# Two Swin blocks on one core: transposes in P's banks, a bank for hidden pieces, the second MLP product two steps later

## The chip, the core and the metric

The program runs on one NeuronCore of a Trainium2 chip. TensorE (PE) multiplies and transposes, VectorE (DVE), ScalarE (ACT) and GpSimd (POOL) work on elements, and the SP queue starts the DMAs. Each engine takes its own instructions in order and waits on semaphores for the others. The metric is device time in microseconds, lower is better.

## What is computed

The input is 32 images of 192 channels and 32 x 32 pixels. Two Swin blocks follow each other: layer 0 with a shift of 4, a relative bias and a mask, layer 1 with the same shift and without bias and mask. Cut to its core:

```python
def block(x, shift, bias, mask):                 # x: (B, H, W, 192)
    h = layer_norm(x)
    h = roll(h, (-4, -4))
    q, k, v = split_heads(windows(h, 8) @ qkv_w + qkv_b)       # 12 heads of 16
    a = softmax(q @ k.T * 16 ** -0.5 + bias + mask)
    x = x + roll(unwindows(a @ v @ proj_w + proj_b), (4, 4))
    h = layer_norm(x)
    return x + gelu(h @ fc1_w + fc1_b) @ fc2_w + fc2_b         # hidden width 768
```

## The kernel before

**Tiles.** A tile is 128 tokens, two windows. An image has 8 tiles, and with two layers over 32 images there are 512 tile steps. They go in groups of four; `group_order` lists the groups, so that groups of layer 0 and layer 1 alternate. Most operands are kept as a high and a low fp16 part: an engine writes the high part and VectorE or GpSimd subtracts it from the full value for the low part. So the second product is 18 matmuls (6 hidden blocks, three pairs of parts), and `x2` or `x5` in a row is a set of such parts.

**Steps.** There is no scheduler. `run(slot)` calls each engine's own `slot(s)` for s from -6 to beyond 512, and in it the functions stand in the order in which that engine does them. Function `f(s - 2)` in slot s means that the tile two steps older is meant. In a step TensorE does: P.V of tile s-2, the v product of tile s, scores of s, projection of s-3, the transposes of P of s-1, the subtraction of the row maximum from the scores of s (`shift_scores`), the q/k product of s+3. ScalarE copies v and q/k high, takes exp, copies P high. VectorE does the row maximum, the attention residual, statistics, v low, P low, q/k low. GpSimd does the normalising, the parts of o and the image order. SP does the DMA transposes, loads and stores.

**The MLP.** It works on a whole group of four tiles, LATE = 8 steps behind. `mlp_phase(s)` gives the phase p (a group) and the place 0 to 3 of a step in it. The first product makes six hidden pieces of 128 rows by 512 tokens (`hidden(m)`, line 587, five matmuls each), four at the end of place 0 and two at the head of place 1, so 30 matmuls in a row. They alternate between the two banks of `ps_s`, which the attention scores also use; piece 0 waits for exp of the same step (`exp_done`), and piece m >= 2 for gelu of piece m-2. ScalarE does gelu (line 723), GpSimd the high part of it (line 1137), VectorE the low part (line 968). The second product (`mlp_out`, lines 600 and 602) is done tile by tile: tile 0 in place 1, tiles 1 and 2 in place 2, tile 3 in place 3, and each is followed by VectorE's residual (line 955). Tile 1's stands in ps_o, the others in ps_v, the bank of the v product. The first of them waits for the low part of piece six (`h_lo`).

**PSUM.** Eight banks: `ps_tr` for the x and y transposes, `ps_o` for P.V, `ps_qk` for q/k and projection, `ps_v`, two of `ps_s`, and two of `ps_t` for the transposes of P. Before the gelus and after them ScalarE loads a table (lines 734 and 729).

**Where a bank is shared**, a wait on its last reader stands in front of the writer. For ps_v in `v_product`:

```python
if place == 1 or p < 0 or p == 0 == place:
    ge("v_lo", n - 1)
else:
    ge("resid2", p * GROUP + (-1, None, 0, 2)[place])
```

`ge(name, n)` waits until event `name` has come for item n.

Of the kernel before, what the change touches and what calls it, by code (L numbers as in the profile page):

```python
# [140 lines left out]
def swin_program(nc, x, layers, rel_bias, ident_in, q_mask_in, k_mask_in, out):  # L141
    H2 = C // 2
    with ExitStack() as ctx:
# [10 lines left out]
        ps_tr, ps_o, ps_qk, ps_v = banks  # L154
# [60 lines left out]
        hid16 = sb("hid16", [128, 2, HC, GROUP * TOK], F16)  # L215
# [76 lines left out]
        def _(sp):  # L292
# [71 lines left out]
            def slot(s):  # L364
# [42 lines left out]
                for n, places in ((s - LATE - 2, (0, 1)), (s - LATE - 6, (2, 3))):  # L407
                    if live(n) and visit(n)[1] == 1 and n % GROUP in places:
                        ge("y_ready", rank(n) | 1)
                        store(visit(n)[0], visit(n)[2])  # L410
# [10 lines left out]
        def _(pe):  # L421
# [29 lines left out]
            def slot(s):  # L451
# [3 lines left out]
                def take_tr(reader, n):  # L455

                    ge(*tr_reader)
                    tr_reader[:] = [reader, n]

# [8 lines left out]
                def x_transpose(n):  # L468

                    _, layer, t = visit(n)  # L470
                    take_tr("x_in", rank(n))
                    ge("x_ordered", rank(n))
                    for k in range(2):
                        last = nc.tensor.transpose(ps_tr[:, k * H2:(k + 1) * H2], x_win[:, k, t * TOK:(t + 1) * TOK],
# [27 lines left out]
                def rel_scores(n):  # L502

                    _, layer, t = visit(n)
                    if place == 1:
                        ge("gelu", p * HC + HC - 1)
# [31 lines left out]
                def p_transpose(n):  # L538


                    ge("p_lo", n - 1)
                    ge("exp_done", n)
# [5 lines left out]
                def pv_product(n):  # L548


                    if mlp and place == 3:
                        ge("resid2", p * GROUP + 1)
                    else:
                        ge("o_norm", n - 1)
# [21 lines left out]
                def hidden(m):  # L576
# [3 lines left out]
                    if m == 0:  # L580
                        for n in range(p * GROUP, (p + 1) * GROUP):
                            landed(pe, "xh_in", n + AHEAD)
                        ge("exp_done", min(s, ENDS))
                    if m >= 2:
                        ge("gelu", u - 2)
                    for i, (part, blk) in enumerate(((0, 0), (3, 0), (2, 2), (1, 1), (4, 1))):
                        last = mm(ps_s[:, u % 2, :].rearrange("p (a t) -> p a t", a=GROUP),  # L587
# [4 lines left out]
                def mlp_out(n, bank):  # L592
# [3 lines left out]
                    if n % GROUP == 0:  # L596
                        ge("h_lo", p * HC + HC - 1)
# [625 lines left out]
```

## Time and profile before

| | |
|---|---|
| median of 3 runs | 4226.17 us (4218.26 to 4227.47) |
| the profiled execution | 4221.89 us, of which the span is 4220.1 us |
| busy: TensorE, VectorE, GpSimd, ScalarE | 92%, 81%, 73%, 64% of the span |
| granted TensorE clock | 1.0 in the mean, 9 tenths or more in all 40 slices |

A timeline row gives the start, the busy time and what ran. TensorE's rows are pipelined: one begins before the end of the last is over, so the time that a set takes is read from one start to the next. The same holds for VectorE, by less. Between groups of four steps the pattern repeats, with small differences between groups of layer 0 and of layer 1: the bias product (line 510) and the x transposes (line 474) come with layer 0, the y transposes (line 609) with the tiles that leave layer 1.

### The profile page before, as it was taken

The numbers are of one execution on the slowest core, as the hardware profiler recorded it, in microseconds if no ns is written. First come the engines' busy times: TensorE is split into PE (matmuls) and PEld (weight loads), VectorE is DVE, ScalarE is ACT, GpSimd is POOL, SyncE is SP. The second block draws the span as 40 slices with busy tenths as digits, with TensorE's granted clock in tenths as the row PEclk, the third lists the DMA queues.
The fourth block names the chain that finished last, engine by engine and source line by source line (L and its number), as shares of the span: only waits on it lengthen the run. The fifth ranks groups of instructions, "written<-read, shape, count | busy, mean of one in ns | idle before, by whom it ended". The sixth has DMA issues, their size and how long they took to land. (4 is left out here: it accounts for less than half of the span.)

```text
span 4220.1 us, 173918 instructions
## 1 busy us (share of the span) xinstructions
PE 3900.1 (92%) x65872; PEld 2870.6 (68%) x65872; DVE 3430.2 (81%) x9093; ACT 2692.4 (64%) x5409; POOL 3085.5 (73%) x6257
## 2 busy tenths in 40 slices
PE   4999999999999999999999999999999999999998
PEld 2667667766766766766676676667666766766765
DVE  6888888888888888888888888888888888888885
ACT  1666666666666666666666666666666666666665
POOL 4777777777777777777777777777777777777775
PEclk9999999999999999999999999999999999999999
DMA  4644545445554554555546555445544555544543
GB/s 104 108 95 101 103 98 101 104 100 99 103 103 97 104 101 98 103 99 104 98 101 103 99 100 100 104 96 105 102 96 103 101 102 100 100 103 96 95 98 63
DMA packets 1545145, 421.00 MB, mean 100 GB/s; under 512 B 1441782, under 2 KB 1542522, under 8 KB 1544316
## 3 DMA queue, kind: packets, MB, share of 16 engines
q1 hardware_dynamic: 1540732, 409.87, 49.9%
q8 instruction: 528, 8.65, 0.9%
q14 instruction: 301, 2.47, 0.2%
q10 hardware_dynamic: 3584, 0.01, 0.0%
HBM read 32.15 MB, written 25.17 MB: 14 GB/s over the span
## 5 line engine op out<-in xcount | busy, mean ns | idle before, releaser
L968 DVE TENSOR_TENSOR hid<-scaled,hid 128x512 f16<-128x512 f32 x768 | 674.1, 891 | 344.9 <-POOL hid L1137 325.5
L600 PE MATMUL bank<-w_fc,hid 128*128 128x192 f16 x9216 | 845.4, 246 | 106.9 <-DVE hid L968 104.8
L587 PE MATMUL ps_s<-xh,w_fc 128*128 128x512 f16 x3840 | 859.2, 379 | 70.9 <-ACT stage L709 64.5
L1074 POOL TENSOR_TENSOR rstd<-vare,half 128x2 f32<-128x2 f32 x520 | 360.6, 693 | 770.1 <-DVE vare L908 770.1
L600 PEld LDWEIGHTS bank<-w_fc,hid 128*128 128x128 f16 x9216 | 761.4, 98 | 195.9 <-DVE v_blk L924 169.6
L587 PEld LDWEIGHTS ps_s<-xh,w_fc 128*128 128x128 f16 x3840 | 355.5, 97 | 560.5 <-issue 110.9
L1137 POOL TENSOR_SCALAR hid<-scaled 128x512 f16<-128x512 f32 x768 | 564.7, 739 | 121.8 <-ACT scaled L723 120.9
L723 ACT ACTIVATE scaled<-ps_s,b_fc 128x512 f32<-128x512 f32 x768 | 529.3, 689 | 154.5 <-PE ps_s L587 133.7
L690 ACT ACTIVATE xs<-xn 128x192 f16<-128x192 f32 x512 | 185.7, 363 | 683.2 <-POOL xn L1081 683.2
L715 ACT ACTIVATE pt<-ps_t 128x768 f16<-128x768 f32 x512 | 415.7, 812 | 303.8 <-PE ps_t L544 300.7
L463 PE MATMUL bank<-w_qkv,xh 128*128 128x384 f16 x2560 | 501.0, 326 | 6.1 <-DMA xh<-xs 3.6
L709 ACT ACTIVATE stage<-ps_s 128x768 f32<-128x768 f32 x512 | 417.4, 815 | 134.6 <-PE ps_s L533 134.6
L930 DVE TENSOR_REDUCE smax<-ps_s 128x12 bf16<-128x768 f32 x512 | 488.3, 954 | 16.8 <-PE ps_s L524 1.5
L935 DVE TENSOR_TENSOR pt<-ps_t,pt 128x768 f16<-128x768 f32 x512 | 489.6, 956 | 12.1
L696 ACT ACTIVATE qk<-bank 128x768 f16<-128x768 f32 x512 | 419.7, 820 | 9.7 <-PE bank L463 9.7
L704 ACT ACTIVATE v_blk<-bank 64x192 f16<-64x192 f32 x1024 | 333.7, 326 | 137.2 <-PE bank L496 131.0
L561 PEld LDWEIGHTS bank<-v_blk,pt 128*64 128x64 f16 x18432 | 333.0, 112 | 128.8 <-issue 95.9
L544 PE MATMUL ps_t<-ident,stage 128*128 128x128 f32 x3072 | 419.7, 273 | 0.1
L914 DVE SCALAR_TENSOR_TENSOR qk<-bank,qk 128x192 f16<-128x192 f32 x1024 | 315.8, 350 | 91.7 <-ACT qk L696 88.8
L561 PE MATMUL bank<-v_blk,pt 128*64 128x34 f16 x18432 | 383.5, 185 | 5.0 <-DVE pt L935 4.7
L463 PEld LDWEIGHTS bank<-w_qkv,xh 128*128 128x128 f16 x2560 | 244.6, 97 | 180.2 <-DVE x_tok L955 8.3
L924 DVE SCALAR_TENSOR_TENSOR v_blk<-bank,v_blk 64x192 f16<-64x192 f32 x1024 | 357.0, 349 | 7.1
(113 smaller groups left out, 7182.7 us busy)
## 6 DMA issues: line engine op xcount, KB each, us to landing
x_img<-in_x_dram SPq DMA_DIRECT2D x256, 96.0 KB, 2.2
out_dram<-y_img SPq DMA_DIRECT2D x256, 96.0 KB, 2.0
xh<-xs SPq DMA_TRANSPOSE x520, 2.5
qkt<-qk SPq DMA_TRANSPOSE x512, 3.3
ot<-os SPq DMA_TRANSPOSE x512, 2.3
stage<-in_L_conv_fc_w_dram SPq DMA_DIRECT2D x2, 384.0 KB, 4.3
stage<-in_L_conv_w_fc_dram SPq DMA_DIRECT2D x2, 384.0 KB, 4.2
stage<-in_L_conv_qkv_w_dram SPq DMA_DIRECT2D x2, 288.0 KB
```

The source lines that it names most:

```text
L463: last = mm(dst, blocks[:, blk, :], w[:, part, n0:n1], start=(i == 0), stop=(i == 4 and bias is None))
L544: last = nc.tensor.transpose(ps_t[:, g // 3, (g % 3) * TOK:(g % 3 + 1) * TOK], p_tok[:, n % 2, g].rearrange("p a k -> p (a k)"), ident[:, :])
L561: last = mm(ps_o[rows, g * 2 * VW:(g + 1) * 2 * VW].rearrange("p (a d) -> p a d", a=2), pt[:, n % 2, ps, g, rows], v_blk[:, n % 2, vs, :, ...
L587: last = mm(ps_s[:, u % 2, :].rearrange("p (a t) -> p a t", a=GROUP), w_fc1[layer][:, part, m * 128:(m + 1) * 128], xh[:, p % 2 * GROUP:(p ...
L600: mm(bank[:, 0:C], hid16[:, hs, m, tok], w_fc2[layer][:, ws, m, :], start=(m == 0 and i == 0), stop=False)
L696: copy(hi_places(n), src.broadcast_to([128, 2, HEADS, 2, HD]), ACT.Copy, scale=UNSCALE)\
L709: nc.scalar.activation(p_tok[:, n % 2].rearrange("p g a k -> p a g k"), ps_s[:, :, 0:PAIRS * WIN].rearrange("p a (g k) -> p a g k", g=PAIR ...
L723: nc.scalar.activation(hid[:, u % 4, :], ps_s[:, u % 2, :], ACT.Gelu, bias=b_fc1[layer][:, m:m + 1], scale=UNSCALE).then_inc(S["gelu"], 1)
L930: v.tensor_reduce(smax[:, n % 2], ps_s[:, :, 0:PAIRS * WIN].rearrange("p a (g k) -> p a g k", g=PAIRS), AX.X, ALU.max).then_inc(S["max_don ...
L935: v.tensor_tensor(pt[:, n % 2, 1].rearrange("p (b g) t -> p b (g t)", b=2), ps_t[:, :, 0:3 * TOK], pt[:, n % 2, 0].rearrange("p (b g) t -> ...
L968: v.tensor_tensor(hid16[:, 1, m, :], hid[:, u % 4, :], hid16[:, 0, m, :], ALU.subtract)\
L1137: g_.tensor_scalar(hid16[:, 0, m, :], hid[:, u % 4, :], 1.0, 0.0, ALU.mult, ALU.add)\
```

## The change

- `ps_tr` is gone as a bank for transposes. The x transposes now write P's first bank (`ps_x`), the y transposes P's second (`ps_y`). They wait until P's low part of the step before is made, and P's transposes wait for their readers in turn.
- The freed bank `ps_hid` takes hidden pieces 0 and 5; pieces 1 to 4 alternate in `ps_s`. Piece 0 no longer waits for exp, piece 1 does. Pieces 0 to 2 stand at the end of place 0, pieces 3 to 5 in place 1 behind P.V and v.
- The second product of tile n is in step n + 10 (`OUT = LATE + 2`), one in every step, always in ps_v; its residual opens VectorE's next step. So `v_product` waits for the residual of the step before in every place. `hid16` becomes two buffers, the second in the memory of the weight stage.
- VectorE's statistics of the attention output, both aggregates and the centring stand together behind v low; in place 1 P's low part comes before them. Low parts of hidden pieces 0 to 4 are in place 1, of piece 5 in place 2.
- ScalarE copies x and y at the head of the step; its q/k copy comes before gelu 0.
- The group order begins each round with layer 0 instead of layer 1, and the stores are in one place, four steps after the second product.

```diff
+OUT = LATE + 2
...
-        order += [(image - 2, 1, 0), (image, 0, 0), (image - 2, 1, 1), (image, 0, 1)]
+        order += [(image, 0, 0), (image - 2, 1, 0), (image, 0, 1), (image - 2, 1, 1)]
...
-        ps_tr, ps_o, ps_qk, ps_v = banks
+        ps_hid, ps_o, ps_qk, ps_v = banks
+        hid_banks = [ps_hid[:, :], ps_s[:, 0, :], ps_s[:, 1, :], ps_s[:, 0, :], ps_s[:, 1, :], ps_hid[:, :]]
+        ps_x = ps_t[:, 0, 0:C]
+        ps_y = ps_t[0:H2, 1, 0:2 * TOK].rearrange("p (k t) -> p k t", k=2)
...
@@ TensorE, x_transpose
-                    take_tr("x_in", rank(n))
+                    ge("p_lo", min(n - 8, ENDS))
+                    ge("x_in", rank(n) - 1)
...
@@ v_product
-                    if place == 1 or p < 0 or p == 0 == place:
+                    if n <= OUT:
                         ge("v_lo", n - 1)
                     else:
-                        ge("resid2", p * GROUP + (-1, None, 0, 2)[place])
+                        ge("resid2", n - OUT - 1)
...
@@ hidden
+                        ge("gelu", u - 1)
+                    if m == 1:
                         ge("exp_done", min(s, ENDS))
-                    if m >= 2:
-                        ge("gelu", u - 2)
+                    if m >= 3:
+                        ge("gelu", u - (2, 2, 5)[m - 3])
...
@@ mlp_out
                     if n % GROUP == 0:
-                        ge("h_lo", p * HC + HC - 1)
+                        ge("h_lo", n // GROUP * HC + HC - 1)
+                    ge("v_lo", min(s, ENDS))
+                    ge("resid2", n - 1)
...
@@ y_transpose
-                    take_tr("y_ready", rank(n))
+                    ge("p_lo", min(s - 2, ENDS))
+                    ge("y_ready", rank(n) - 1)
...
@@ TensorE's step
-                if mlp and place == 1:
-                    hidden(4)
-                    hidden(5)
                 if live(s + 6) and visit(s + 6)[1] == 0:
                     x_transpose(s + 6)
+                if live(s - OUT - 2) and visit(s - OUT - 2)[1] == 1:
+                    y_transpose(s - OUT - 2)
                 if live(s) and place != 1:
                     rel_scores(s)
                 if live(s - 2):
                     pv_product(s - 2)
                 if live(s):
                     v_product(s)
+                if mlp and place == 1:
+                    for m in range(3, HC):
+                        hidden(m)
...
                 if live(s + 3):
                     qk_product(s + 3)
+                if live(s - OUT):
+                    mlp_out(s - OUT)
                 if mlp and place == 0:
                     for m in range(3):
                         hidden(m)
...
@@ VectorE's step
+                if live(s - OUT - 1):
+                    mlp_residual(s - OUT - 1)
...
-                if mlp and place == 1:
-                    hidden_lo(5)
...
+                if mlp and place == 1:
+                    hidden_lo(4)
+                if mlp and place == 1 and live(s - 1):
+                    p_lo(s - 1)
+                if mlp and place == 2:
+                    hidden_lo(5)
```

TensorE, a group whose tiles are of layer 1, from the q/k product of place 0 to that of place 1. Names: `ps_s<-xh,w_fc` hidden pieces, `bank<-v_blk,pt` P.V, `bank<-w_qkv,xh 64x96` v, `bank<-w_fc,hid` the second product. Before:

```order
L463 MATMUL bank<-w_qkv,xh 128x384 x5
L587 MATMUL ps_s<-xh,w_fc 128x512 x30
L474 MATMUL bank<-ident,x_win 128x96 x2
L561 MATMUL bank<-v_blk,pt 64x34 x36
L496 MATMUL bank<-w_qkv,xh 64x96 x20
L524 MATMUL ps_s<-qkt 64x64 x24
L463 MATMUL bank<-w_proj,ot 128x192 x5
L465 MATMUL bank<-b_out,bias_rows 128x192
L544 MATMUL ps_t<-ident,stage 128x128 x6
L533 MATMUL ps_s<-smax,neg_ident 128x384 x2
```

And after:

```order
L607 MATMUL bank<-w_fc,hid 128x192 x18
L609 MATMUL bank<-b_out,bias_rows 128x192
L592 MATMUL bank<-xh,w_fc 128x512 x5
L592 MATMUL ps_s<-xh,w_fc 128x512 x10
L476 MATMUL ps_t<-ident,x_win 128x96 x2
L564 MATMUL bank<-v_blk,pt 64x34 x36
L498 MATMUL bank<-w_qkv,xh 64x96 x20
L592 MATMUL ps_s<-xh,w_fc 128x512 x10
L592 MATMUL bank<-xh,w_fc 128x512 x5
L526 MATMUL ps_s<-qkt 64x64 x24
```

The thirty matmuls are two sets of fifteen with the x transposes, P.V and v between them, and a second product stands ahead of the first set.

VectorE, one plain step from the MLP residual (`x_tok<-bank`) to the q/k low part; `smax` is the row maximum, `mv` and `bn` the statistics, `nmean` and `vare` the centring, `pt` P's low part. Before:

```order
L955 SCALAR_TENSOR_TENSOR x_tok<-bank,x_tok 128x192
L888 BN_STATS bn<-x_tok 128x6
L894 BN_AGGR mv<-bn 128x2
L941 RECIPROCAL o_inv<-bank 128x12
L948 TENSOR_TENSOR o_tok<-bank,o_inv 128x192
L930 TENSOR_REDUCE smax<-ps_s 128x12
L955 SCALAR_TENSOR_TENSOR x_tok<-bank,x_tok 128x192
L888 BN_STATS bn<-x_tok 128x6
L924 SCALAR_TENSOR_TENSOR v_blk<-bank,v_blk 64x12x16 x2
L894 BN_AGGR mv<-bn 128x2
L907 TENSOR_SCALAR nmean<-mv 128x2
L908 TENSOR_SCALAR vare<-mv 128x2
```

And after:

```order
L871 BN_STATS bn<-x_tok 128x6
L938 SCALAR_TENSOR_TENSOR x_tok<-bank,x_tok 128x192
L924 RECIPROCAL o_inv<-bank 128x12
L931 TENSOR_TENSOR o_tok<-bank,o_inv 128x192
L913 TENSOR_REDUCE smax<-ps_s 128x12
L938 SCALAR_TENSOR_TENSOR x_tok<-bank,x_tok 128x192
L907 SCALAR_TENSOR_TENSOR v_blk<-bank,v_blk 64x12x16 x2
L871 BN_STATS bn<-x_tok 128x6
L877 BN_AGGR mv<-bn 128x2 x2
L890 TENSOR_SCALAR nmean<-mv 128x2
L891 TENSOR_SCALAR vare<-mv 128x2
```

The statistics that stood behind the MLP residual now stand ahead of it, and the first aggregate went from there to behind v low.

## Rows read from the trace of the kernel before

**Rows 1.** The page: span, and each engine's busy time and share.
```profile
span 4220.1 us, 173918 instructions
...
PE 3900.1 (92%) x65872; PEld 2870.6 (68%) x65872; DVE 3430.2 (81%) x9093; ACT 2692.4 (64%) x5409; POOL 3085.5 (73%) x6257
```

**Rows 2.** TensorE's timeline: start us, busy us, engine line op, tiles, count [idle before].
```profile
1999.58 6.71 PE L587 MATMUL ps_s<-xh,w_fc 128*128 128x512 f16 x30 [0.56 <-ACT stage L709]
...
2063.61 6.71 PE L587 MATMUL ps_s<-xh,w_fc 128*128 128x512 f16 x30 [0.56 <-ACT stage L709]
```

**Rows 3.** The page's groups by line: busy, mean ns, idle before them.
```profile
L968 DVE TENSOR_TENSOR hid<-scaled,hid 128x512 f16<-128x512 f32 x768 | 674.1, 891 | 344.9 <-POOL hid L1137 325.5
L600 PE MATMUL bank<-w_fc,hid 128*128 128x192 f16 x9216 | 845.4, 246 | 106.9 <-DVE hid L968 104.8
```

**Rows 4.** TensorE's timeline, one plain step (place 3 to place 0).
```profile
2021.59 0.60 PE L496 MATMUL bank<-w_qkv,xh 128*64 128x96 f16 x20
2022.12 0.38 PE L524 MATMUL ps_s<-qkt 64*64 64x64 f16 x24
...
2023.59 0.38 PE L609 MATMUL bank<-ident,x_tok 128*96 128x128 f32 x2
2023.81 0.49 PE L533 MATMUL ps_s<-smax,neg_ident 128*128 128x384 bf16 x2
...
2024.95 1.65 PE L600 MATMUL bank<-w_fc,hid 128*128 128x192 f16 x18
...
2026.52 0.49 PE L510 MATMUL ps_s<-bias_tab,pair_ident 128*128 128x384 f16 x2
2026.94 0.75 PE L561 MATMUL bank<-v_blk,pt 128*64 128x34 f16 x36
2027.53 0.60 PE L496 MATMUL bank<-w_qkv,xh 128*64 128x96 f16 x20
```

**Rows 5.** VectorE's timeline in the same step.
```profile
2021.11 0.36 DVE L955 SCALAR_TENSOR_TENSOR x_tok<-bank,x_tok 128x192 f32<-128x192 f32 x1 [0.32 <-PE bank L602]
2021.38 0.35 DVE L888 BATCH_NORM_STATS2 bn<-x_tok 128x6 f32<-128x192 f32 x1
...
2022.56 0.96 DVE L930 TENSOR_REDUCE smax<-ps_s 128x12 bf16<-128x768 f32 x1
...
2023.82 0.36 DVE L888 BATCH_NORM_STATS2 bn<-x_tok 128x6 f32<-128x192 f32 x1
2024.10 0.71 DVE L924 SCALAR_TENSOR_TENSOR v_blk<-bank,v_blk 64x192 f16<-64x192 f32 x2
2024.84 0.18 DVE L894 BATCH_NORM_AGGREGATE mv<-bn 128x2 f32<-128x6 f32 x1
...
2025.19 0.16 DVE L908 TENSOR_SCALAR vare<-mv 128x2 f32<-128x2 f32 x1
2025.38 0.96 DVE L935 TENSOR_TENSOR pt<-ps_t,pt 128x768 f16<-128x768 f32 x1
2026.49 0.62 DVE L914 SCALAR_TENSOR_TENSOR qk<-bank,qk 128x192 f16<-128x192 f32 x2
2027.03 0.35 DVE L955 SCALAR_TENSOR_TENSOR x_tok<-bank,x_tok 128x192 f32<-128x192 f32 x1
```

**Rows 6.** ScalarE's timeline: gelu six, exp's table load, P's copy.
```profile
2006.32 0.69 ACT L723 ACTIVATE scaled<-ps_s,b_fc 128x512 f32<-128x512 f32 x1 [0.39 <-PE ps_s L587]
...
2008.30 1.28 ACT L729 ACT_TABLE_LOAD   x1
...
2009.82 0.81 ACT L715 ACTIVATE pt<-ps_t 128x768 f16<-128x768 f32 x1
```

**Rows 7.** VectorE's timeline: the last hidden low part of a group.
```profile
2011.11 0.69 DVE L968 TENSOR_TENSOR hid<-scaled,hid 128x512 f16<-128x512 f32 x1
```

**Rows 8.** GpSimd's rstd and ScalarE's copy of xn, timelines of each.
```profile
2018.85 0.69 POOL L1074 TENSOR_TENSOR rstd<-vare,half 128x2 f32<-128x2 f32 x1 [1.37 <-DVE vare L908]
...
2021.28 0.36 ACT L690 ACTIVATE xs<-xn 128x192 f16<-128x192 f32 x1 [0.75 <-POOL xn L1081]
```

More of the change, by code:

```diff
@@ L406, in slot @@
                     load(visit(s + 9)[0] + 1, visit(s + 9)[2])
[L407 to L410, printed above, removed]
+                n = s - OUT - 4
+                if live(n) and visit(n)[1] == 1:
+                    ge("y_ready", rank(n) | 1)
+                    store(visit(n)[0], visit(n)[2])
             run(slot)
@@ L548, in pv_product @@
                 def pv_product(n):
[L551 to L554, printed above, removed]
+                    ge("o_norm", n - 1)
                     ge("v_lo", n)
@@ L722, in gelu @@
                     ge("h_lo", u - 4)
-                    nc.scalar.activation(hid[:, u % 4, :], ps_s[:, u % 2, :], ACT.Gelu, bias=b_fc1[layer][:, m:m + 1],
+                    nc.scalar.activation(hid[:, u % 4, :], hid_banks[m], ACT.Gelu, bias=b_fc1[layer][:, m:m + 1],
                                          scale=UNSCALE).then_inc(S["gelu"], 1)
@@ L742, in y_evac @@
                             act.wait_ge(y_stored[h], 16 * image)
-                    tile = ps_tr[0:H2, 0:2 * TOK].rearrange("p (k t) -> p k t", k=2)
-                    for win, img in box_pairs(t, tile, y_img[:, :, :]):
+                    for win, img in box_pairs(t, ps_y, y_img[:, :, :]):
                         last = copy(img, win, ACT.Copy)
@@ L763, in slot @@
                 if mlp and place == 1:
+                    for m in range(3, HC):
+                        gelu(m)
                     load_exp()
@@ L776, in slot @@
                     load_gelu()
-                    gelu(0)
                 if live(s + 3):
@@ L780, in slot @@
                 if mlp and place == 0:
+                    gelu(0)
                     gelu(1)
-                if last_block and place == 2:
-                    y_evac(p * GROUP + 1)
             run(slot)
@@ L959, in attention_residual, with mlp_residual @@
                     residual(n, ps_qk[:, 0:C], stream(n, 1), stream(n, 0), "pr", "resid1")
-                def mlp_residual(n, bank):
-                    residual(n, bank[:, 0:C], token_rows(n), stream(n, 1), "fc2", "resid2")
+                def mlp_residual(n):
+                    residual(n, ps_v[:, 0:C], token_rows(n), stream(n, 1), "fc2", "resid2")
                 def hidden_lo(m):
@@ L1143, in slot @@
                     norm1_lo(s + 4)
[L1144 to L1145 removed]
                 if live(s - 4):
                     norm2_lo(s - 4)
+                if mlp and place == 1:
+                    hidden_hi(3)
                 if live(s + 3):
                     set_mask(s + 3)
[L1150 to L1151 removed]
                 if live(s - 2):
@@ L1154, in slot @@
                     o_lo(s - 2)
+                if mlp and place == 1:
+                    hidden_hi(4)
+                    hidden_hi(5)
                 if live(s + 10) and visit(s + 10)[1] == 0 and s + 10 >= TILES:
@@ L1163, in slot @@
                 if mlp and place == 0:
-                    for m in range(4):
+                    for m in range(3):
                         hidden_hi(m)
```

103 lines of the change are left out of this document (35 added, 68 removed).

## The prediction, made before the changed kernel was run

> **What bounds the kernel now.** I read the page's busy shares first. TensorE is busy for 92% of the span and VectorE for 81% [rows 1], which looks like a TensorE kernel that can win 8% at most. The share hides where each waits, so the timeline comes next. The starts of the six hidden pieces repeat every 64.0 us per two groups (1999.58 to 2063.61) [rows 2]. TensorE idles 0.56 us before the first piece, for exp. The groups by line show that the second product (L600) waited 104.8 us for VectorE's low part of the hidden layer, 0.8 us in each of 128 groups [rows 3].
>
> Then one plain step, a step without hidden pieces. On TensorE it runs from one v product to the next, 2021.59 to 2027.53, 5.94 us [rows 4]. On VectorE the same step, from one MLP residual to the next, takes 5.92 us (2021.11 to 2027.03) and has next to no gap in it [rows 5]. So here VectorE is a second bound, as tight as TensorE. They are tied in a ring through the bank ps_v: residual, v product, scores, row maximum, the rest of VectorE's step, next residual. The price of the change is decided in this ring.
>
> **What the change takes away.** In a group TensorE stood 0.56 us before piece one (the exp), 0.8 us before the first L600. Now piece one has a bank of its own and a second product stands before it, and the second product comes two steps later. Both waits go: 1.4 us a group, 87 us over 62 pairs of groups, if nothing else were late. No matmul, activation or VectorE operation is added or dropped; the steady numbers of each stay.
>
> **What is late next.** I walk one group on the new order, from the start of the row maximum in place 0.
>
> Stretch A, to the end of piece six, is TensorE's. Row maximum to the subtraction of it 1.00 (0.96 plus a handover); subtraction and q/k product 1.14 (2023.81 to 2024.95); second product with bias 1.57 (2024.95 to 2026.52) [rows 4]; three pieces 3.27, half of the 6.71 for six less an end of 0.17 [rows 2]; a transpose pair 0.22 (2023.59 to 2023.81), which I take for x too; P.V 0.59; v 0.53; three more pieces 3.27. Sum 11.59. The gelus finish behind: piece four needs gelu two, with P.V and v between as cover, so I put no wait here. If that cover failed, gelu's 0.69 would show.
>
> Stretch B, from there to the row maximum of place 2, is no longer TensorE's. ScalarE must do gelu six, load exp's table and then copy P before VectorE can take P's low part. Handover 0.20 and gelu 0.69; 1.54 from its end to P's copy (load at 2008.30, copy at 2009.82); copy 0.81 [rows 6]; handover 0.03. VectorE: P low 0.88 to the next start, its 0.96 less the 0.08 by which back-to-back operations overlap (0.36 at 2023.82, next start 2024.10); statistics, two aggregates and centring 1.00 (that 0.28, then 0.54 from the aggregate at 2024.84 to P low at 2025.38, and 0.18 for the second aggregate, which now stands beside the first); q/k low 0.54 (2026.49 to 2027.03); statistics 0.28; residual 0.36 and handover 0.06; v, scores and handover 0.97 (2021.59 to 2022.56) [rows 4, 5]. Sum 7.36. TensorE's own work in B up to v is about 4.8 to 5.7, so it waits about 0.7 to 1.6 in front of v. Before, the gelus stood a whole first half of a step earlier and this was hidden. The removed waits thus come back at another place.
>
> Stretch C, place 2 to place 3, is the ring plus hidden piece six on VectorE. The ring costs more than before. Row maximum and attention residual 1.26 (2022.56 to 2023.82), v low 0.74, statistics to centring 1.00, P low 0.88, q/k low 0.54, statistics 0.28, residual and handover 0.42, then 0.97 to the next row maximum: 6.09 [rows 5]. Before it was 5.92, since statistics for a later tile (2021.38) stood behind the residual and, with an aggregate, filled the time in which VectorE waited for v and scores. Now it stands in front of the residual, and only reciprocal and normalisation fill that hole. That is 0.17 a step. Low part six is in the ring in place 2: alone it takes 0.61 to the next start (2011.11, busy 0.69) [rows 7]. The mean of all 768 is 0.89 [rows 3]; those beside GpSimd work are the long ones. In B the centring came late, so GpSimd's chain of place 2 (o high, o low) falls upon it. Bounds are 0.61 and 0.89; I take 0.89, nearer to the mean. C is 6.98.
>
> What the row shows is a low part that grows by 0.20 beside GpSimd, on average over all. The Trainium skill, "SBUF — State Buffer", "Who interferes with whom", says more: a VectorE instruction with two SBUF inputs and a GpSimd instruction that reads SBUF lock each other out for the whole instruction. By that rule low part six might stand a whole GpSimd operation longer and C would be some 0.3 longer. The sum goes without it.
>
> Stretch D, place 3 to place 0, is the plain ring, 6.09.
>
> A group is 11.59 + 7.36 + 6.98 + 6.09 = 32.02. Every second group adds something. Where the tiles are of layer 0, TensorE has x pair, y pair, bias and P.V (0.22 + 0.22 + 0.42 + 0.59, the bias from 2026.52 to 2026.94) between P's low part and v [rows 4], since both transposes now wait in P's bank for that low part. With a handover 1.5 against VectorE's 1.17 for q/k low, statistics and residual: +0.4 in place 3 and +0.1 in place 0. The x transposes were free of that wait before. So a pair is 64.54 against 64.03, +0.51 over 62 pairs (some 125 of the 128 groups run in the steady state), +32 us. Warm-up gets the same wait in some eight steps, and the tail has two more steps but the same four second products behind the last low part: together I take +3, between 0 and +8. The profiled execution took 4221.9 us (span 4220.1) [rows 1], so the sum is 4257. The median of the three runs is 4226.2, 0.1% above that execution; I say 4258.
>
> Also moved: the store on SP's queue comes four steps after the second product for all places, and GpSimd's hidden part four goes from place 0 to place 1. SP's stores wait on y that ScalarE made in the step before, and nothing behind them on SP is needed for more than a step. Piece four's high part has VectorE's earlier low parts beside it. I cost both at nothing; if GpSimd were late, the row maximum in place 1 would show it. ScalarE's q/k copy now stands behind the gelu table load in place 0; VectorE then idles over 1 us there, but A belongs to TensorE in that time.
>
> One more rule bears on B. The row shows the table load at 2008.30 and P's copy 1.52 later [rows 6]. The Trainium skill, "ScalarE: Activation LUTs", "What ACT_TABLE_LOAD costs", adds a drain of about 1.38 us to each switch. With it B would be 1.4 longer, +170 us in all; the trace has no such gap between the load and the copy, and the measurement decides.
>
> **Rivals.**
>
> (1) The ring takes 6.09, but low part six runs alone (0.61). A pair is 0.56 less, 63.98: 4222 - 3 + 3 = 4222. For it: in every second group GpSimd has no image work then. Against: its o low comes right there. This is "no change".
>
> (2) Faster. TensorE keeps what the removed waits give, because VectorE's moved pieces cost nothing: ring 5.92 in C and D as in the trace, low part six alone, so 63.98 - 4 x 0.17 = 63.3 a pair, -0.73 x 62 + 3 = -42: 4180. For it: VectorE has 19% idle, and it has no more to do than before. Against: that idle lies in places 0 and 1, where it is not the bound. It decides if the row maximum in a plain step starts sooner than 6.0 after the last.
>
> (3) Slower still. In place 2 ScalarE's copy of xn (L690) stands before v's copy. It came 2.43 us after GpSimd's rstd started (2018.85 to 2021.28) [rows 8]. Centring in place 1 now comes behind P low, so I compare two paths from the last centring operation to v low in place 2. VectorE's: 0.19 + 0.54 + 0.28 + 0.42 + 0.97 + 1.26 = 3.66 [rows 5]. The other: about 0.3 to rstd, 2.43, xn's copy 0.3 and v's two copies 0.6 (estimates from the 0.36 of xn's), 3.6 to 3.7: no slack. If GpSimd is later by 0.3, v low and all behind it is later by 0.3: +0.6 a pair, +37 us, 4295.
>
> (4) The change doesn't take effect as told: banks or order coincide with the old ones. The order lists show that they don't; under 1 in 50.
>
> **Chances and range.** Forecast 4258 (4235 to 4275): 0.42. Rival 1: 0.20. Rival 2, with in-between sizes: 0.22. Rival 3: 0.16. A measurement of this kernel can tell about 0.2%, 8 us, from no change. From the cases: faster by more than that 0.25, within it 0.20, slower 0.55. The range 4178 to 4302 takes in rivals 1 and 3 and nearly all of 2.
>
> **What would show it.** The wait of the second product for the hidden low part falls from 104.8 to under 80 us and sits in place 2; the wait of piece one for exp is gone. PEld or TensorE waits for the MLP residual in front of v grow to about 1 us per group in place 2, and plain steps take 6.1 us on VectorE. In the six-piece stretch there is no gap over 0.2. VectorE's low part six in place 2 shows whether 0.69 or 0.96. I am wrong if plain steps come under 6.0, or if v in place 2 starts before 6.2 after the last piece's end.

## The result, and the profile after

The changed kernel took 4242.39 us (median of 4 runs, 4241.56 to 4242.92) against 4224.76 for the kernel before: a ratio of 1.0044, 95% interval 1.0026 to 1.0061. The forecast was slower, 4258, range 4178 to 4302. The direction held, and so did the mechanism in its main terms; the size came out 16 us smaller. Three of the signs named beforehand failed. Two are the "I am wrong if" thresholds, both crossed by a little: a plain step comes at 5.98 us (under 6.0), and v in place 2 starts 6.10 us after the last piece's end (under 6.2). The third failed plainly: the second product waits for the hidden low part more than before, not less. (Pieces one to six are `hidden(0)` to `hidden(5)` here, as in the prediction.)

The page of the kernel after, its span, busy shares and four groups by line; they answer [rows 1] and [rows 3].

```profile
span 4241.1 us, 174413 instructions
...
PE 3931.5 (93%) x65872; PEld 2899.8 (68%) x65872; DVE 3377.8 (80%) x9093; ACT 2688.4 (63%) x5409; POOL 3111.0 (73%) x6257
...
L913 DVE TENSOR_REDUCE smax<-ps_s 128x12 bf16<-128x768 f32 x512 | 490.2, 957 | 147.8 <-PE ps_s L526 136.4
...
L607 PE MATMUL bank<-w_fc,stage 128*128 128x192 f16 x4608 | 422.7, 246 | 60.1 <-DVE stage L951 58.7
L607 PE MATMUL bank<-w_fc,hid 128*128 128x192 f16 x4608 | 422.7, 246 | 58.6 <-DVE hid L951 58.0
...
L907 DVE SCALAR_TENSOR_TENSOR v_blk<-bank,v_blk 64x192 f16<-64x192 f32 x1024 | 363.2, 355 | 35.6 <-ACT v_blk L697 28.8
```

The counts of each engine's operations are those of before: no work was added. The wait of the second product is 58.7 + 58.0 = 116.7 us (before 104.8), and two waits are new in size: VectorE's row maximum waits 136.4 us for the scores (1.5 before), and v's low part 28.8 us for ScalarE's copy of v. Two rows of the waits view (who <- for whom: us in all, times, longest):

```profile
PE bank L498 <- DVE x_tok L938: 77.5, 135, 1.3
DVE v_blk L907 <- ACT v_blk L697: 28.8, 123, 1.0
```

The first is v's product waiting for the MLP residual. To see which of these lie on the path, one reads VectorE's row maxima. A row maximum (L930 before, L913 after) can start only when both engines have come round, so its starts cut the pair of groups into eight stages. VectorE's timeline of the kernel before, the stages from place 2 to place 3 and from place 3 to place 0 in both groups:

```profile
2913.26 0.96 DVE L930 TENSOR_REDUCE smax<-ps_s 128x12 bf16<-128x768 f32 x1
2920.66 0.96 DVE L930 TENSOR_REDUCE smax<-ps_s 128x12 bf16<-128x768 f32 x1
2926.60 0.96 DVE L930 TENSOR_REDUCE smax<-ps_s 128x12 bf16<-128x768 f32 x1
...
2945.57 0.96 DVE L930 TENSOR_REDUCE smax<-ps_s 128x12 bf16<-128x768 f32 x1
2953.03 0.96 DVE L930 TENSOR_REDUCE smax<-ps_s 128x12 bf16<-128x768 f32 x1
2958.73 0.96 DVE L930 TENSOR_REDUCE smax<-ps_s 128x12 bf16<-128x768 f32 x1
```

And of the kernel after, one whole pair, with the idle time before each in brackets:

```profile
2911.91 0.96 DVE L913 TENSOR_REDUCE smax<-ps_s 128x12 bf16<-128x768 f32 x1
2924.43 0.96 DVE L913 TENSOR_REDUCE smax<-ps_s 128x12 bf16<-128x768 f32 x1 [0.56 <-PE ps_s L526]
2930.66 0.96 DVE L913 TENSOR_REDUCE smax<-ps_s 128x12 bf16<-128x768 f32 x1 [0.20 <-PE ps_s L526]
2938.21 0.96 DVE L913 TENSOR_REDUCE smax<-ps_s 128x12 bf16<-128x768 f32 x1
2944.19 0.96 DVE L913 TENSOR_REDUCE smax<-ps_s 128x12 bf16<-128x768 f32 x1 [0.26 <-PE ps_s L526]
2956.33 0.96 DVE L913 TENSOR_REDUCE smax<-ps_s 128x12 bf16<-128x768 f32 x1 [0.23 <-PE ps_s L526]
2962.88 0.96 DVE L913 TENSOR_REDUCE smax<-ps_s 128x12 bf16<-128x768 f32 x1 [0.46 <-PE ps_s L526]
2970.05 0.96 DVE L913 TENSOR_REDUCE smax<-ps_s 128x12 bf16<-128x768 f32 x1 [0.46 <-PE ps_s L526]
2976.23 0.96 DVE L913 TENSOR_REDUCE smax<-ps_s 128x12 bf16<-128x768 f32 x1
```

The same starts, read between 2890 and 2990 us in each kernel and subtracted (the last column is the sum, a pair of groups). Stage 0-1 and 1-2 together are the prediction's A and B, 2-3 is C, 3-0 is D.

| kernel | 0-1 | 1-2 | 2-3 | 3-0 | 0-1 | 1-2 | 2-3 | 3-0 | pair |
|---|---|---|---|---|---|---|---|---|---|
| before | 12.17 | 6.31 | 7.40 | 5.94 | 12.16 | 6.81 | 7.46 | 5.70 | 63.95 |
| after | 12.52 | 6.23 | 7.55 | 5.98 | 12.14 | 6.55 | 7.17 | 6.18 | 64.32 |
| e1_stat | 12.51 | 6.10 | 7.67 | 5.81 | 12.14 | 6.28 | 7.18 | 6.23 | 63.92 |
| e2_vfirst | 12.52 | 6.22 | 6.96 | 5.97 | 12.14 | 6.54 | 6.69 | 6.17 | 63.21 |
| e3_bias | 12.52 | 6.22 | 7.23 | 5.98 | 12.14 | 6.55 | 7.18 | 5.97 | 63.79 |
| e4_all | 12.52 | 6.11 | 6.70 | 5.83 | 12.14 | 6.29 | 6.80 | 5.93 | 62.32 |
| e5_twice5 | 12.52 | 6.22 | 8.17 | 5.97 | 12.14 | 6.54 | 7.89 | 6.17 | 65.62 |
| e9_spare | 12.52 | 6.49 | 7.57 | 5.98 | 12.14 | 6.82 | 7.19 | 6.17 | 64.88 |
| e8_before_v | 11.89 | 6.35 | 7.40 | 5.94 | 12.00 | 6.82 | 7.45 | 5.70 | 63.55 |

(Starts are rounded, so a stage may be 0.01 off. In the kernel before and in e8_before_v, the halves may stand the other way round; only their sums are compared. One stretch can mislead: over 60 pairs of each trace the median stages are within 0.02 of these rows in all but two places. The 6.80 of e4_all is rare, the median there is 6.35; and where e1_stat has 6.23 the median is 6.17.) From before to after, stages 0-1 and 1-2 together stay at 37.45 and 37.44, the 2-3 stages give 0.14 back, and the plain stages 3-0 lose 0.52: 11.64 becomes 12.16. That is the answer to "where did the time go". In 0-1 and 1-2 the gone waits (0.56 for exp, 0.8 for the low part) pay for most of a second product, 1.57, that has moved to place 0. In 2-3 TensorE has one second product less, but VectorE's ring does not let the stage shrink by more than 0.07. In 3-0, where nothing was to be won, the ring is longer. The means over 60 pairs say the same: -0.05 in 0-1 and 1-2, -0.18 in 2-3, +0.52 in 3-0.

Two stretches lie outside the pairs. The first hidden piece starts at 146.42 us instead of 140.92, so the warm-up costs 5.5. The last block of hidden pieces starts at 4217.80, and the end comes 23.3 us later; before, it was 23.4 (4196.73 to 4220.1). The tail is unchanged:

```profile
4217.80 1.24 PE L592 MATMUL bank<-xh,w_fc 128*128 128x512 f16 x5
```

The 127 groups between these two starts take 4071.4 us instead of 4055.8, 15.6 more. With the 5.5 this is the 21.0 by which the two profiled spans differ; the medians of the runs differ by 17.6.

### The profile page after: what moved, and what is told of

Same layout as the page of the kernel before. It is cut to its first block, busy times and chain, and to the rows that moved or that the text cites. A ratio compares the mean times of both kernels' runs of the same rounds, so it can differ in the third digit from the quotient of the medians.

```text
span 4241.1 us, 174413 instructions
## 1 busy us (share of the span) xinstructions
PE 3931.5 (93%) x65872; PEld 2899.8 (68%) x65872; DVE 3377.8 (80%) x9093; ACT 2688.4 (63%) x5409; POOL 3111.0 (73%) x6257
## 4 chain that ended last, share of the span: by engine, by line
PE 57%; DVE 15%; ACT 11%; issue 9%; POOL 4%; DVEq 0%; DMA 0%; POOLq 0%; SPq 0%; ACTq 0%
PE ps_s L592 13%; PE bank L607 9%; PE bank L464 7%; PE bank L592 6%; PE bank L564 5%; PE bank L498 4%; PE ps_t L550 4%; ACT L722 4%; DVE pt L918 3%; DVE bn L871 2%; ACT scaled L716 2%; ACT pt L708 2%; POOL rstd L1059 2%; PE ps_s L526 2%; PE ps_s L535 2%
## 5 line engine op out<-in xcount | busy, mean ns | idle before, releaser
L913 DVE TENSOR_REDUCE smax<-ps_s 128x12 bf16<-128x768 f32 x512 | 490.2, 957 | 147.8 <-PE ps_s L526 136.4
L592 PE MATMUL ps_s<-xh,w_fc 128*128 128x512 f16 x2560 | 595.6, 380 | 0.0
L683 ACT ACTIVATE xs<-xn 128x192 f16<-128x192 f32 x512 | 186.5, 364 | 627.1 <-POOL xn L1066 627.0
L716 ACT ACTIVATE scaled<-ps_s,b_fc 128x512 f32<-128x512 f32 x512 | 351.7, 687 | 216.0 <-PE ps_s L592 216.0
L607 PE MATMUL bank<-w_fc,stage 128*128 128x192 f16 x4608 | 422.7, 246 | 60.1 <-DVE stage L951 58.7
L607 PE MATMUL bank<-w_fc,hid 128*128 128x192 f16 x4608 | 422.7, 246 | 58.6 <-DVE hid L951 58.0
L607 PEld LDWEIGHTS bank<-w_fc,stage 128*128 128x128 f16 x4608 | 382.5, 98 | 109.7 <-DVE stage L951 83.2
L607 PEld LDWEIGHTS bank<-w_fc,hid 128*128 128x128 f16 x4608 | 382.7, 98 | 108.2 <-DVE hid L951 82.4
L592 PEld LDWEIGHTS ps_s<-xh,w_fc 128*128 128x128 f16 x2560 | 240.1, 98 | 280.1
L689 ACT ACTIVATE qk<-bank 128x768 f16<-128x768 f32 x512 | 409.8, 800 | 10.6 <-PE bank L464 10.5
L951 DVE TENSOR_TENSOR stage<-scaled,stage 128x512 f16<-128x512 f32 x384 | 318.4, 829 | 110.7 <-POOL stage L1122 65.0
L951 DVE TENSOR_TENSOR hid<-scaled,hid 128x512 f16<-128x512 f32 x384 | 312.2, 813 | 106.0 <-POOL hid L1122 64.3
L907 DVE SCALAR_TENSOR_TENSOR v_blk<-bank,v_blk 64x192 f16<-64x192 f32 x1024 | 363.2, 355 | 35.6 <-ACT v_blk L697 28.8
```

Source lines behind the costliest of these rows:

```text
L592: last = mm(hid_banks[m].rearrange("p (a t) -> p a t", a=GROUP), w_fc1[layer][:, part, m * 128:(m + 1) * 128], xh[:, p % 2 * GROUP:(p % 2 ...
L607: mm(ps_v[:, 0:C], hid16[n // GROUP % 2][:, hs, m, tok], w_fc2[layer][:, ws, m, :], start=(m == 0 and i == 0), stop=False)
L689: copy(hi_places(n), src.broadcast_to([128, 2, HEADS, 2, HD]), ACT.Copy, scale=UNSCALE)\
L716: nc.scalar.activation(hid[:, u % 4, :], hid_banks[m], ACT.Gelu, bias=b_fc1[layer][:, m:m + 1], scale=UNSCALE).then_inc(S["gelu"], 1)
L913: v.tensor_reduce(smax[:, n % 2], ps_s[:, :, 0:PAIRS * WIN].rearrange("p a (g k) -> p a g k", g=PAIRS), AX.X, ALU.max).then_inc(S["max_don ...
L951: v.tensor_tensor(hid16[p % 2][:, 1, m, :], hid[:, u % 4, :], hid16[p % 2][:, 0, m, :], ALU.subtract)\
```

## Experiments

Each is an edit of the changed kernel, except the last. Differences to it are differences of medians, and each ratio is to the kernel before, timed beside it. The kernel before had medians of 4221.9 to 4224.8 us in these timings, so a difference of 3 us says nothing.

**Where VectorE's statistics stand (e1_stat).**

```diff
@@ VectorE's step
                 if live(s - OUT - 1):
                     mlp_residual(s - OUT - 1)
+                if live(s + 5):
+                    statistics(s + 5, 0)
...
-                if live(s + 6):
-                    statistics(s + 6, 0)
```

> One part of the change undone on VectorE: the statistics for a later tile stand behind the MLP residual again, as before, so the residual starts some 0.27 us sooner and the hole in front of the row maximum is filled. Theory A (VectorE's ring residual - v - scores - row maximum sets places 2 and 3): each ring gets 0.27 us shorter where q/k low and residual come last, that is in four of six ring steps per pair of groups (not where transposes and bias stand between P low and v): about -1.1 us a pair, -60 to -70 us, 4175 to 4185 us. Theory B (TensorE sets the steps, VectorE's order is slack): within 5 us of the changed kernel, 4242.

Measured: 4217.43 us, ratio 0.9987 (0.9978 to 0.9997), 25 us less than the changed kernel. The sign and the mechanism are right: row maxima wait 74.3 us for scores instead of 136.4, and the plain step without transposes goes from 5.98 to 5.81, the 0.17 of the prediction (this run's own expectation said 0.27 a ring). The size was missed: 4217 lies between both theories. In the table, 1-2 gains 0.40 over both groups, but 2-3 gives 0.13 of it back and the 3-0 stage with transposes gains nothing. The reason for the first is in VectorE's timeline of e1_stat, place 2:

```profile
2944.91 0.96 DVE L913 TENSOR_REDUCE smax<-ps_s 128x12 bf16<-128x768 f32 x1 [0.20 <-PE ps_s L526]
...
2946.61 0.73 DVE L907 SCALAR_TENSOR_TENSOR v_blk<-bank,v_blk 64x192 f16<-64x192 f32 x2 [0.47 <-ACT v_blk L697]
```

v's low part waits 0.47 for ScalarE's copy, where it waited 0.22 in the changed kernel (in all 52.8 us against 28.8), and the stage takes 7.18 where 0.17 less than 7.17 was to be had. What VectorE saves before the row maximum it spends in front of v. So there is a third path, and it hangs on ScalarE's order.

**ScalarE's order in a step (e2_vfirst).** The copy of v (L697) goes ahead of the copy of xn (L683), which waits for GpSimd.

```diff
@@ ScalarE's step
+                if live(s):
+                    v_hi(s)
                 if live(s - 4):
                     norm2_hi(s - 4)
-                if live(s):
-                    v_hi(s)
```

> ScalarE makes v's high part before its copy of xn. Theory A (rival 3 of the prediction at work: in place 2 v low waits for v's copy, which stands behind the copy of xn, 28.8 us in total in the trace): the wait goes, -20 to -30 us, 4212 to 4222 us. Theory B (the wait is covered, since the end of that step is set by the transposes behind P low): within 5 us of 4242.

Measured: 4183.11 us, ratio 0.9908 (0.9893 to 0.9923), 59 us less, twice what was expected. The table puts all of it in stage 2-3: 7.55 to 6.96 and 7.17 to 6.69. ScalarE's timeline of the changed kernel and then of e2_vfirst, place 2 of a group:

```profile
2963.37 0.36 ACT L683 ACTIVATE xs<-xn 128x192 f16<-128x192 f32 x1 [3.10 <-POOL xn L1066]
2963.64 0.65 ACT L697 ACTIVATE v_blk<-bank 64x192 f16<-64x192 f32 x2
```

```profile
2063.01 0.67 ACT L697 ACTIVATE v_blk<-bank 64x192 f16<-64x192 f32 x2 [1.00 <-PE bank L498]
2063.82 0.36 ACT L683 ACTIVATE xs<-xn 128x192 f16<-128x192 f32 x1
```

In the first, ScalarE idles 3.10 us for GpSimd and cannot take v, which has long been in its bank when xn comes; v's copy ends at 2964.29, and VectorE has waited 0.22 for it. In the second, v's copy ends 0.34 after the row maximum of its step has begun (2063.34). So v's low part starts 0.26 after the attention residual instead of 0.56, which gives back 0.30. The other half goes with contention, and VectorE's and GpSimd's timelines show it. First the changed kernel (GpSimd, then VectorE), then e2_vfirst (VectorE, then GpSimd):

```profile
2030.72 0.55 POOL L1095 TENSOR_TENSOR os<-o_tok,os 128x192 f16<-128x192 f32 x1
```

```profile
2030.07 0.73 DVE L907 SCALAR_TENSOR_TENSOR v_blk<-bank,v_blk 64x192 f16<-64x192 f32 x2 [0.22 <-ACT v_blk L697]
2030.84 0.98 DVE L951 TENSOR_TENSOR hid<-scaled,hid 128x512 f16<-128x512 f32 x1
```

```profile
2064.47 0.72 DVE L907 SCALAR_TENSOR_TENSOR v_blk<-bank,v_blk 64x192 f16<-64x192 f32 x2
2065.23 0.69 DVE L951 TENSOR_TENSOR hid<-scaled,hid 128x512 f16<-128x512 f32 x1
```

```profile
2065.42 0.91 POOL L1095 TENSOR_TENSOR os<-o_tok,os 128x192 f16<-128x192 f32 x1
```

In the changed kernel GpSimd's o part is under way (since 2030.72) when low part six starts at 2030.84, and low part six takes 0.98. In e2_vfirst GpSimd comes at the same point of the step, but v's low part is 0.30 earlier, so VectorE is first, by 0.19 us, and takes 0.69. GpSimd's operation is now the longer one (0.91 instead of 0.55), where nobody waits for it. This is the rule and not one group: low part six takes about 0.98 in 125 of the 128 groups of the changed kernel (0.69 in all 128 of the kernel before) and 0.69 in 126 of e2_vfirst. So a wait of 0.22 had cost 0.5 to 0.6 us, once in every group of 32 us. The second product's waits for that low part fall from 116.7 to 21.4 + 20.4 = 41.8 us.

**TensorE's order in front of v (e3_bias).** Bias ahead of the transposes that wait for P's low part.

```diff
@@ TensorE's step
+                if live(s) and place != 1:
+                    rel_scores(s)
                 if live(s + 6) and visit(s + 6)[1] == 0:
                     x_transpose(s + 6)
                 if live(s - OUT - 2) and visit(s - OUT - 2)[1] == 1:
                     y_transpose(s - OUT - 2)
-                if live(s) and place != 1:
-                    rel_scores(s)
```

> TensorE does the bias product of layer 0 before the x and y transposes, which wait for P low; the bias product doesn't. Theory A (in place 3 of layer 0 groups, and by a little in place 0, the work between P low and v sets the step): 0.42 us less in one step and 0.1 us in another per pair of groups, -25 to -32 us, 4210 to 4217 us. Theory B (the MLP residual comes last there too): within 5 us of 4242.

Measured: 4209.96 us, ratio 0.9972 (0.9961 to 0.9983), 32 us less. Two stages changed, 7.55 to 7.23 and 6.18 to 5.97, together the 0.53 of the pair. This is the term "+0.4 in place 3 and +0.1 in place 0" measured, as 0.32 and 0.21; its sum was right, and it came only from the order of the two functions.

**All three (e4_all).**

> The three edits at once: statistics behind the residual, v's high part before the copy of xn, bias before the transposes. Theory A: with the bias out of the way the residual is last in more steps, so the parts add up to at least their sum, about -2 us a pair of groups: 4110 to 4140 us, faster than both kernels. Theory B (something behind them, the exp table load or the matmuls themselves, takes over): less than two thirds of the sum of the single gains.

Measured: 4117.51 us (4114.29 to 4117.92), ratio 0.975 (0.9736 to 0.9765). It is 125 us below the changed kernel; the three alone sum to 117. They help each other: in most pairs the second 2-3 stage is 6.35 where e2_vfirst has 6.69, and with the bias out of the way the second 3-0 stage goes from 6.18 to 5.93. How much of this each edit gives was not separated. Part of the gain is lost again. The median stages add up to 61.86, the mean pair is 62.40, and nearly all of the difference lies in the 0-1 and 3-0 stages of some groups, where TensorE's projection now waits for the DMA of o (`ot<-os`): 26.7 us in 59 waits, against 1.3 us in 3 in the changed kernel. The page of e4_all:

```profile
PE 3890.1 (95%) x65872; PEld 2901.9 (71%) x65872; DVE 3346.8 (81%) x9093; ACT 2731.4 (66%) x5409; POOL 3137.1 (76%) x6257
```

This beats both kernels, by 2.5% and 2.9%. What the change removed is 104.8 us of waits for the low part [rows 3] and 64.5 us for exp, this row of the waits view of the kernel before:

```profile
PE ps_s L587 <- ACT stage L709: 64.5, 117, 0.6
```

Together 169 us, of which e4_all keeps 104 (4117.51 against 4221.86 for the kernel before, timed beside it). So the removed waits were worth something; the three orders of instructions around them cost 125.

**One low part doubled, in place 2 and in place 1 (e5_twice5, e6_twice0).** The same VectorE operation is done twice, once into a spare tile. For piece six it stands in the ring, for piece one in a place where VectorE waits anyway.

```diff
+        twice = sb("twice", [128, GROUP * TOK], F16)
...
@@ hidden_lo, e5_twice5 (in e6_twice0 the condition is m == 0)
+                    if m == 5:
+                        v.tensor_tensor(twice[:, :], hid[:, u % 4, :], hid16[p % 2][:, 0, m, :], ALU.subtract)
```

> VectorE does the low part of hidden piece six twice, in place 2; the second result goes to a spare tile. Nothing else changes and the output stays. Theory A (place 2 is VectorE's ring, and whatever is added there is paid in full): 0.6 to 0.95 us in each of 128 groups, +77 to +120 us over the changed kernel's 4242: 4320 to 4362 us. Theory B (VectorE's 20% idle absorbs it): under +15 us.

> The same doubling for the low part of piece one, at the head of place 1. Theory A (the stretch up to the row maximum of place 1 is TensorE's, VectorE waits there 0.5 us or so three times): under +15 us, 4242 to 4257 us. Theory B (VectorE is the bound throughout): +77 us or more, as for piece six.

Measured: 4328.76 us, ratio 1.0254 (1.0239 to 1.0269), 86 more than the changed kernel; and 4245.16 us, ratio 1.0058 (1.0041 to 1.0075), 3 more. The groups of e5_twice5 (VectorE, by line) and then of e6_twice0, 64 of each of two names:

```profile
L953 DVE TENSOR_TENSOR twice<-scaled,hid 128x512 f16<-128x512 f32 x64 | 62.4, 975 | 1.9
```

```profile
L953 DVE TENSOR_TENSOR twice<-scaled,hid 128x512 f16<-128x512 f32 x64 | 44.6, 698 | 31.6 <-POOL hid L1125 31.6
```

Equal work on the same engine costs 86 us in place 2 and 3 in place 1. In place 2 the stages grow by 0.62 and 0.72 (8.17 and 7.89). That is less than the 0.98 that its row shows. Of the two low parts in a row only the first takes 0.98; the second takes 0.68 and 0.77 in turn, 0.60 and 0.69 to the next start, and that is what the added one costs. This shows that VectorE's chain sets the time in place 2, and that its 20% of idle time lies elsewhere.

**ScalarE's chain behind the gelus (e9_spare).** Stretch B was forecast as ScalarE's and VectorE's, not TensorE's. Three more one-element activations stand between the table load and P's copy.

```diff
-        spare = sb("spare", [1, 2], F32)
+        spare = sb("spare", [1, 8], F32)
...
@@ load_exp
+                    for i in range(2, 5):
+                        nc.scalar.activation(spare[:, i:i + 1], half[0:1, :], ACT.Exp)
```

> ScalarE does three more one-element exps after the table load of place 1, which delays its copy of P by about 0.1 us each. Theory A (stretch B is set by gelu six, table load and P's copy): the delay is paid in full, 0.3 us in each of 128 groups, +30 to +45 us over 4242: 4272 to 4287 us. Theory B (VectorE's low parts or TensorE set stretch B): under +10 us.

Measured: 4279.30 us, ratio 1.0137 (1.0122 to 1.0152), 37 more. ScalarE's timeline of the changed kernel, then of e9_spare, in place 1:

```profile
2955.99 0.69 ACT L716 ACTIVATE scaled<-bank,b_fc 128x512 f32<-128x512 f32 x1 [0.39 <-PE bank L592]
2956.70 1.28 ACT L722 ACT_TABLE_LOAD   x1
...
2958.10 0.78 ACT L708 ACTIVATE pt<-ps_t 128x768 f16<-128x768 f32 x1
```

```profile
2004.40 1.28 ACT L723 ACT_TABLE_LOAD   x1
2005.69 0.39 ACT L723 ACTIVATE spare<-half 1x1 f32<-1x1 f32 x3
...
2006.08 0.78 ACT L708 ACTIVATE pt<-ps_t 128x768 f16<-128x768 f32 x1
```

P's copy starts 1.68 us after the table load instead of 1.40. The 0.28 shows in full: stage 1-2 grows by 0.26 and 0.27, and 128 x 0.28 = 36 us. The chain of B goes through ScalarE's table load and P's copy, with no slack at all.

**The wait for exp (e7_expwait).** Piece one (`hidden(0)`) waits for exp again, though it has its own bank.

```diff
@@ hidden
                         ge("gelu", u - 1)
-                    if m == 1:
                         ge("exp_done", min(s, ENDS))
```

> The wait of hidden piece one for exp is put back, though its bank doesn't need it. Theory A (the second product that now stands in front of the pieces covers the exp anyway, so the bank of its own removes nothing more): within 5 us of the changed kernel, 4242. Theory B (the free bank is what took the 0.56 us a group away): up to +72 us.

Measured: 4245.64 us, ratio 1.0057 (1.0042 to 1.0072), 3 more than the changed kernel, which is not told from none; its stages 0-1 take 12.14 and 12.52 again. So it was not the freedom of its bank from exp that removed the 0.56 us; the second product, 1.57 us that now stands ahead of piece one, covers exp.

**A like edit on the kernel before (e8_before_v).** ScalarE's copy of v ahead of xn's. In this kernel the copy of xn stood further up, so the edit also puts it behind gelus five and six and the copy of x in place 1.

```diff
@@ ScalarE's step, kernel before
-                if live(s - 4):
-                    norm2_hi(s - 4)
                 if mlp and place == 1:
                     gelu(4)
                     gelu(5)
...
                 if live(s):
                     v_hi(s)
+                if live(s - 4):
+                    norm2_hi(s - 4)
```

> The kernel before, with one edit that gained 59 us on the changed kernel: ScalarE makes v's high part before its copy of xn. Theory A (that queueing is a side effect of the change, which moved the centring behind P low in place 1; in the kernel before v low hardly waited, 7 us in all): within 8 us of before, 4222 to 4226. Theory B (the edit is good by itself): 1% faster here too, about 4180 us.

Measured: 4226.85 us against 4222.54, ratio 1.001 (1.0000 to 1.0019): no gain in time. In the stages 2-3, where the edit gave 0.59 and 0.48 in the changed kernel, it gives nothing here (7.40 and 7.45). So that cost was made by the change, which put the centring in place 1 behind P's low part and so made xn late.

But the edit is not idle here. The median 0-1 stages are 0.28 and 0.16 shorter. In the groups shown below, GpSimd waits for xn's copy before its low part of xn, so that operation no longer falls beside VectorE's hidden low part four. VectorE in the kernel before and in e8_before_v, then GpSimd and TensorE in e8_before_v:

```profile
2007.70 0.95 DVE L968 TENSOR_TENSOR hid<-scaled,hid 128x512 f16<-128x512 f32 x1 [0.29 <-POOL hid L1137]
```

```profile
2009.49 0.69 DVE L968 TENSOR_TENSOR hid<-scaled,hid 128x512 f16<-128x512 f32 x1 [0.29 <-POOL hid L1137]
```

```profile
2010.54 0.55 POOL L1115 TENSOR_TENSOR xs<-xn,xs 128x192 f16<-128x192 f32 x1 [1.15 <-ACT xs L690]
```

```profile
2063.87 0.57 PE L463 MATMUL bank<-w_proj,ot 128*128 128x192 f16 x5 [0.66 <-DMA ot<-os]
```

The last row is what takes the gain away again. GpSimd's parts of o come later too (10.46 us after the start of piece one instead of 9.71), and TensorE's projection waits for their DMA: 23.0 us in 33 waits, against 1.8 in one. The median stages add up to 63.55 instead of 63.95, but the mean pair is 64.07, against 64.13. That the late parts of o make the DMA late is read from these rows, not tested.

## Why the prediction was right, and where not

**A, 11.59.** Right. From the row maximum at 2944.19 to the end of piece six. That end is gelu six's start less the handover of 0.20: 2955.99 - 0.20 = 2955.79, so 11.60. TensorE's timeline of the changed kernel has no bracket in it:

```profile
2947.93 1.24 PE L592 MATMUL bank<-xh,w_fc 128*128 128x512 f16 x5
2949.01 2.32 PE L592 MATMUL ps_s<-xh,w_fc 128*128 128x512 f16 x10
...
2954.71 1.24 PE L592 MATMUL bank<-xh,w_fc 128*128 128x512 f16 x5
```

The gelus were hidden, as costed.

**B, 7.36.** Right in kind, too long by 0.27. Measured 2955.79 to 2962.88, 7.09. The mis-sized terms: gelu six to P's copy took 2.11, not 0.69 + 1.54 (the same table load was followed by P's copy 1.52 after its start before, and 1.40 now; the rows don't show why); and the statistics up to the centring took 0.90 where 1.00 was taken, since q/k low starts 0.07 behind `vare`, where 0.19 was read for P's low part. The rest agrees within some 0.03 a term. v's product does wait for the residual, 0.98, as said "about 1 us a group in place 2":

```profile
2961.89 0.62 PE L498 MATMUL bank<-w_qkv,xh 128*64 128x96 f16 x20 [0.98 <-DVE x_tok L938]
```

The threshold named beforehand was that v starts no sooner than 6.2 after the last piece's end. It was 2961.89 - 2955.79 = 6.10, so this sign failed, by the same mis-sized terms.

**C, 6.98 and 7.38.** Too short by 0.19 and 0.17 (7.17 and 7.55). Here rival 3 came partly true. From the attention residual to v low 0.38 was taken; in D it is 0.27, here 0.57 (2963.75 to 2964.32):

```profile
2963.75 0.35 DVE L938 SCALAR_TENSOR_TENSOR x_mid<-bank,x_new 128x192 f32<-128x192 f32 x1
2964.32 0.73 DVE L907 SCALAR_TENSOR_TENSOR v_blk<-bank,v_blk 64x192 f16<-64x192 f32 x2 [0.22 <-ACT v_blk L697]
2965.08 0.98 DVE L951 TENSOR_TENSOR stage<-scaled,stage 128x512 f16<-128x512 f32 x1
2965.98 0.35 DVE L871 BATCH_NORM_STATS2 bn<-x_mid 128x6 f32<-128x192 f32 x1
```

The prediction called that path "no slack" at a price of 0.3 and gave it 0.16; e2_vfirst confirms the mechanism and shows that the price was 0.5, because the wait also decides who comes first at low part six. That low part took 0.90 to the next start; 0.89 was taken, so rival 1 (0.61) is out in this kernel, and is what e2_vfirst makes true.

**D, 6.09 and 6.19.** Measured 5.98 and 6.18. The claim that a statistics operation on the wrong side of the residual costs 0.17 was right: it came out as 0.17 when undone in the one plain stage without transposes. Before to after the plain stages grew by 0.52 a pair; e3_bias takes 0.21 of that away, e3_bias and e1_stat's edit together (e4_all) 0.40. The level was 0.11 too high, all of it in the 0.38 behind the attention residual. In [rows 5] the operation behind it is a statistics that reads its result; now it is v low, which does not, and it starts after 0.27. "I am wrong if plain steps come under 6.0" was set too tight: one comes at 5.98, against 5.70 for the shortest before, so rival 2 (5.92 kept, pair 63.3) did not come about.

**The sum.** The groups forecast 64.54 a pair; the clean pair shows 64.32: A and B -0.46, C +0.36, D -0.12. Before, the forecast's base of 64.03 holds (63.95 in this stretch). The measured mean over all groups from 5 to 121 rose by 0.28 a pair, from 64.13 to 64.41, and 62 x 0.28 = 17 us, where the forecast had 32. The 0.22 that a pair is under the forecast is B and D, costed too long, less C, costed too short. That these errors partly cancel is luck. The clean pair's +0.37 would be 23; part of the difference is that the kernel before has some pairs with longer 2-3 stages than this one (up to 8.83 instead of 7.40).

One figure beside the sum is wrong. "1.4 us a group, 87 us over 62 pairs" counts the 1.4 once a pair. The two waits come in every group, 104.8 + 64.5 = 169 us in all. The forecast did not use the 87; it was added up from the stretches.

**The wait of the second product.** Wrong: "falls from 104.8 to under 80". It is 116.7. The step that failed is the reading of the removed 0.8 us as a wait that goes. It sits in place 2 now:

```profile
2966.11 1.66 PE L607 MATMUL bank<-w_fc,stage 128*128 128x192 f16 x18 [0.90 <-DVE stage L951]
```

0.90 us in nearly every group. It costs nothing by itself, as far as the rows show: VectorE's residual, which needs this product, waited for TensorE 7 times in the whole run, 12.3 us. TensorE has less to do in place 2 than VectorE, whose ring sets the step, and the idle time has to appear somewhere. The prediction's own sum for C implied it; the sign named for it did not follow from the sum. Before a wait is counted as gone, ask what the engine would wait for next.

**Bank and store.** The moved store, GpSimd's hidden part four and ScalarE's q/k copy were costed at nothing; the stages leave no room for a large term, but none of the three was tested alone. Warm-up and tail together were taken as +3, between 0 and +8, and were +5.5 and -0.1.

**The rule on the shared port.** The rows show low part six at 0.98 when GpSimd started an operation of 0.55 just before it, with 0.43 of that left, and at 0.69 when VectorE started first, by 0.19; then GpSimd's grew from 0.55 to 0.91. The Trainium skill, "SBUF — State Buffer", "Who interferes with whom", says that whoever comes first holds the port and the other blocks. The order agrees with the trace. The amount doesn't quite: a full block would have added 0.43 to VectorE's and the row shows 0.29; it would have added 0.50 to GpSimd's, and the row shows 0.36. **The table load.** P's copy starts 1.40 after the load's start, 0.12 after its end. The drain that the Trainium skill, "ScalarE: Activation LUTs", "What ACT_TABLE_LOAD costs", adds to each switch is not in these rows, and e9_spare shows that a gap there would have been felt in full.

## What to carry to other kernels

When two engines are tied in a ring, cut the timeline at an instruction that both must reach (here the row maximum) and compare the stages; a removed wait counts only in a stage where its engine is the later one. After a change of order, look in every in-order queue for an instruction that waits and has ready work behind it: one copy queued behind another cost 1.4% in the changed kernel, in a stage where the kernel before had no such cost. A total that stays the same can hide a gain and a loss of equal size, as in e8_before_v; the stages show both. Before a change is given up for a small loss, fix what it made late; here three reorderings turned +0.4% into -2.5%.

## What the runs showed of the hardware

- When a VectorE tensor_tensor of 128x512 and a GpSimd operation overlap, the one that starts later is the one that grows: 0.69 to 0.98 us for VectorE, 0.55 to 0.91 for GpSimd, in this kernel's low part six and o part. A start 0.30 us earlier decided which, and was worth 0.29 us a group on the path.
- A one-element activation takes about 0.1 us on ScalarE when others stand behind it (three add 0.28), although a single one's row shows 0.18.
- Four engines showed 95%, 81%, 76% and 66% in the fastest version, 93%, 80%, 73% and 63% in the changed kernel. A share of 80% on VectorE hid a place in which one more low part lengthened the step by 0.62 to 0.72 us.
